# A field-interaction tower: one native product for the mixed tile, another order of the first loads, and two roundings on ScalarE

## What is computed

```python
e = jnp.stack([tbl_f[ids[:, f]] for f in range(39)], axis=1)      # (2048, 39, 16)
x = e
for W in (W0, W1):                                                # (128, 39*39), (128, 128*39)
    inter = (x[:, :, None, :] * e[:, None, :, :]).reshape(B, -1, 16)
    x = jnp.einsum('bid,hi->bhd', inter, W)
    outs.append(x.sum(axis=-1))
h = jnp.concatenate([*outs, dense_ctx], axis=1)                   # 128 + 128 + 16
h = jnp.maximum(h @ W_top1 + b_top1, 0.0)                         # 512
h = jnp.maximum(h @ W_top2 + b_top2, 0.0)                         # 256
y = h @ W_top3
```

## Time and profile before

| | |
|---|---|
| median of 3 runs | 783.21 us (782.36 to 785.63) |
| the profiled execution | 780.78 us, span from first to last instruction 779.0 us |
| TensorE (PE) busy | 696.8 us, 89% of the span |
| VectorE (DVE) busy | 674.9 us, 87% |
| GpSimd (POOL) busy | 501.0 us, 64% |
| ScalarE (ACT) busy | 420.2 us, 54% |
| moved by DMA | 115.67 MB, mean 148 GB/s |

### The profile page before, as it was taken

One profiled execution on the slowest core, in us unless ns is written; L12 is line 12 of the kernel. 1 busy time (PEld: TensorE's weight loads), 2 busy tenths in 40 slices (PEclk: granted clock), 3 DMA queues, 4 the chain that ended last, 5 costly groups with the idle time before them and its releaser, 6 DMA issues.

```text
span 779.0 us, 17028 instructions
## 1 busy us (share of the span) xinstructions
PE 696.8 (89%) x6210; PEld 595.1 (76%) x6210; DVE 674.9 (87%) x864; ACT 420.2 (54%) x769; POOL 501.0 (64%) x406
## 2 busy tenths in 40 slices
PE   0222678999999999999999999999999999999997
PEld 0222455878888888888888888888888888888887
DVE  5653999999999999999999999999999999888810
ACT  0001465656566656557565656655566656575741
POOL 6777887878787877868787887888787850000000
PEclk9999899999999999999999999999999999999999
DMA  4369569696867777787869796777867695854000
GB/s 101 90 156 275 129 184 164 164 171 170 163 167 168 131 185 130 187 134 190 161 163 168 173 162 169 171 148 182 141 171 142 162 160 138 162 153 133 13 7 1
DMA packets 171030, 115.67 MB, mean 148 GB/s; under 512 B 135043, under 2 KB 146906, under 8 KB 170563
## 3 DMA queue, kind: packets, MB, share of 16 engines
q1 hardware_dynamic: 154750, 108.80, 60.3%
q0 software_dynamic: 12800, 3.30, 6.6%
q10 hardware_dynamic: 3397, 2.47, 1.1%
HBM read 104.08 MB, written 15.53 MB: 154 GB/s over the span
## 4 chain that ended last, share of the span: by engine, by line
PE 77%; POOL 7%; DMA 4%; DVE 4%; issue 4%; SPq 3%; ACT 0%; DVEq 0%; ACTq 0%; POOLq 0%
PE z_ps L424 18%; PE x_ps L384 12%; PE x_ps L388 11%; PE x_ps L385 11%; PE g_ps L414 8%; POOL e_rows L360 7%; PE x1T_ps L445 4%; PE aux_ps L373 4%; PE x1T_ps L403 3%; PE x1T_ps L437 2%; SPq L280 2%; PE x1T_ps L435 2%; DVE product_lo L676 2%; DVE products L668 2%; DMA e_scratch<-e_d 2%
## 5 line engine op out<-in xcount | busy, mean ns | idle before, releaser
L360 POOL DMA_INDIRECT e_rows<-in_tbl_dram,ids_sb x400 | 500.6, 1252 | 134.7 <-issue 119.8
L514 ACT CAST product_hi<-products 117x1024 fp32r<-117x1024 f32 (+1 forms) x256 | 242.6, 948 | 102.7 <-DVE products L668 101.7
L676 DVE TENSOR_TENSOR product_lo<-products,product_hi 117x1024 fp32r<-117x1024 f32 (+1 forms) x256 | 277.4, 1084 | 23.1 <-ACT product_hi L514 22.9
L668 DVE TENSOR_TENSOR products<-bases 117x1024 f32<-117x1024 f32 (+1 forms) x256 | 277.5, 1084 | 7.1 <-DMA bases<-eT_scratch 6.5
L384 PE MATMUL x_ps<-product_hi,w_hi 117*128 117x512 f32 x448 | 198.5, 443 | 14.2 <-ACT product_hi L514 10.4
L424 PEld LDWEIGHTS z_ps<-G,w1T 128*128 128x128 f32 x1248 | 165.0, 191 | 17.3 <-issue 0.5
L385 PE MATMUL x_ps<-product_hi,w_lo 117*128 117x512 f32 x448 | 178.2, 398 | 0.0
L424 PE MATMUL z_ps<-G,w1T 128*128 128x128 f32 x1248 | 178.1, 280 | 0.0
L388 PE MATMUL x_ps<-product_lo,w_hi 117*128 117x512 f32 x448 | 148.5, 401 | 19.0 <-DVE product_lo L676 19.0
L388 PEld LDWEIGHTS x_ps<-product_lo,w_hi 117*128 117x128 f32 x448 | 84.3, 190 | 43.6 <-DVE product_lo L676 23.7
L384 PEld LDWEIGHTS x_ps<-product_hi,w_hi 117*128 117x128 f32 x448 | 85.6, 191 | 28.4 <-issue 13.8
(11 more groups left out here) (55 smaller groups left out, 340.1 us busy)
## 6 DMA issues: line engine op xcount, KB each, us to landing
bases<-eT_scratch SPq DMA_DIRECT2D x155, 468.0 KB
e_diag<-e_scratch SPq DMA_DIRECT2D x512, 10.0 KB
id_spread<-id_scratch SPq DMA_DIRECT2D x16, 437.5 KB
e_rows<-in_tbl_dram,ids_sb POOLq DMA_INDIRECT x400
e_scratch<-e_d SPq DMA_DIRECT2D x16, 320.0 KB, 9.5
eT_scratch<-e_rows SPq DMA_DIRECT2D x16, 312.0 KB
eT_scratch<-eT_scratch SPq DMA_DIRECT2D x16, 312.0 KB
w1T<-in_L_rec_W_dram SPq DMA_DIRECT2D x1, 2496.0 KB, 19.3
```

Source lines behind the costliest of these rows:

```text
L360: nc.gpsimd.indirect_dma_start(out=e_rows[t % E_SLOTS][:, f * D:(f + 1) * D], out_offset=None, in_=tables[f], in_offset=bass.IndirectOffse ...
L514: nc.scalar.copy(product_hi[:, first:first + count, :], products[:, first:first + count, :]).then_inc(hi_ready, 1)
L668: nc.vector.tensor_tensor(products[:, first:first + count, :], bases[u % 2][:, b:b + count, cols], bases[u % 2][:, a:a + 1, cols].to_broad ...
L676: nc.vector.tensor_tensor(product_lo[:, first:first + count, :], products[:, first:first + count, :], product_hi[:, first:first + count, : ...
```

## The change

Three edits. (1) Tile 3 is no longer split: its product stays float32 and goes into one float32 matmul with unsplit weights `w_native`, ahead of the other matmuls of group 1; ScalarE's rounding and VectorE's rest of that group shrink to one tile, 512 columns in place of 1024, and `multiply(g, 1)` waits until TensorE has read the product of the chunk before. (2) The first loads: those of chunk 0 are shared by SP (three) and ScalarE's queue (two), and SP issues those of chunk 1 when those of chunk 0 have landed. (3) `copy_e` moves from VectorE to ScalarE, and from the first chunk of the tile before to the end of its third; `store_e` moves in SP's list from chunk `c == 0` to `c == 3`; the rounding of the dense input moves to ScalarE too (`round_dense`). The weights' setup gets one more copy, 117 x 128.

```diff
+NATIVE = 3
...
+def parts_of(n):
+
+    _, _, count, first = GROUPS[n]
+    return slice(first, first + count - (first + count - 1 == NATIVE))
...
-        def load_base_part(queue, t, first, count, ready):
-            for a, starts in enumerate(BASES):
+            for a in range(begin, LOADS, step_of):
+                starts = BASES[a]
...
-            load_base_part(sp, 0, 0, HB // 2, first_ready[0])
+            load_base_part(sp, 0, 0, HB // 2, first_ready[0], 0, 2)
+            sp.wait_ge(first_ready[0], 16 * LOADS)
+            load_base_part(sp, 0, HB // 2, HB // 2, first_ready[1])
             for g in range(CHUNKS):
                 t, c = divmod(g, CPT)
...
                 if c == 0 and t + 1 < TILES:
                     store_eT(t + 1)
+                if c == 3 and t + 1 < TILES:
                     store_e(t + 1)
...
-                _, _, count, first = GROUPS[n]
+                parts = range(NT)[parts_of(n)]
+                if NATIVE == parts.stop:
+                    pe.wait_ge(product_ready, g * NG + n + 1)
+                    nc.tensor.matmul(x1_ps[:, :], w_native[:, :], products[:, NATIVE, :], start=False, stop=False)
                 pe.wait_ge(hi_ready, g * NG + n + 1)
-                for k in range(first, first + count):
+                for k in parts:
                     nc.tensor.matmul(x1_ps[:, :], w0_hi[:, k, :], product_hi[:, k, :], start=(k == 0), stop=False)
...
                 pe.wait_ge(lo_ready, g * NG + n + 1)
-                for k in range(first, first + count):
+                for k in parts:
                     last = nc.tensor.matmul(x1_ps[:, :], w0_hi[:, k, :], product_lo[:, k, :], start=False, stop=(k == NT - 1))
                 last.then_inc(contracted, 1)
...
-                _, _, count, first = GROUPS[n]
                 act.wait_ge(product_ready, g * NG + n + 1)
                 after(act, contracted, (g - 1) * NG + n + 1)
-                nc.scalar.copy(product_hi[:, first:first + count, :], products[:, first:first + count, :]).then_inc(hi_ready, 1)
+                nc.scalar.copy(product_hi[:, parts_of(n), :], products[:, parts_of(n), :]).then_inc(hi_ready, 1)
...
+            def copy_e(t):
+                act.wait_ge(gathered[t % E_SLOTS], (t // E_SLOTS + 1) * 16 * len(GATHERED))
+                act.wait_ge(looked_up, (t + 1) * sum(map(len, SETS)))
+                after(act, e_stored, 16 * t)
+                nc.scalar.copy(e_d[:, :, 0:F], e_rows[t % E_SLOTS][:, :].rearrange("b (f d) -> b d f", d=D)).then_inc(e_d_ready, 1)
+
+            def round_dense(t):
+                act.wait_ge(dense_loaded, (t + 1) * 16 * 3 * GAP // D)
+                after(act, h1_in_ps, M1 * t)
+                nc.scalar.copy(dense_parts[:, :], dense_now[:, :]).then_inc(dense_hi_ready, 1)
...
+            copy_e(0)
             act.wait_ge(eT_doubled, 16)
-            load_base_part(act, 0, HB // 2, HB // 2, first_ready[1])
+            load_base_part(act, 0, 0, HB // 2, first_ready[0], 1, 2)
...
+                if c == 1 and 0 <= t - 2 < TILES - 2:
+                    round_dense(t - 2)
                 if g < CHUNKS:
...
                 if g + 1 < CHUNKS:
                     round_products(g + 1, 1)
+                if c == 2 and t + 1 < TILES:
+                    copy_e(t + 1)
+                if g == CHUNKS - 1:
+                    round_dense(TILES - 2)
+                if g == CHUNKS + CPT:
+                    round_dense(TILES - 1)
...
+                if first + count - 1 == NATIVE:
+                    after(dve, contracted, (g - 1) * NG + n + 1)
                 nc.vector.tensor_tensor(products[:, first:first + count, :], bases[u % 2][:, b:b + count, cols],
...
-                _, _, count, first = GROUPS[n]
-                nc.vector.tensor_tensor(product_lo[:, first:first + count, :], products[:, first:first + count, :],
-                                        product_hi[:, first:first + count, :].bitcast(f32), ALU.subtract).then_inc(lo_ready, 1)
+                nc.vector.tensor_tensor(product_lo[:, parts_of(n), :], products[:, parts_of(n), :],
+                                        product_hi[:, parts_of(n), :].bitcast(f32), ALU.subtract).then_inc(lo_ready, 1)
...
+            nc.vector.tensor_copy(w_native[:, :], w0_sum[:, NATIVE, :]).then_inc(w0_split, 1)
...
-                if c == 0 and t + 1 < TILES:
-                    copy_e(t + 1)
```

More of the change, by code:

```diff
@@ L118, in cin_tower @@
         w0_lo = sb("w0_lo", [R, NT, H], f32r)
+        w_native = sb("w_native", [R, H])
         w1T = sb("w1T", [H, F, H])
@@ L235, in cin_tower, with load_base_part @@
         y_stored = sem("y_stored")
-        def load_base_part(queue, t, first, count, ready):
+        def load_base_part(queue, t, first, count, ready, begin=0, step_of=1):
             at = first % HB * D
-            for a, starts in enumerate(BASES):
+            for a in range(begin, LOADS, step_of):
+                starts = BASES[a]
                 step = starts[1] - starts[0]
@@ L483, in _ @@
                     look_up(t, n)
-            pe.wait_ge(w0_split, 2)
+            pe.wait_ge(w0_split, 3)
             for g in range(CHUNKS + 2 * CPT):
@@ L564, in _ @@
                               w0[j:j + count, 0:halves, shift, :]).then_inc(w0_loaded, 16)
+            copy_e(0)
             act.wait_ge(eT_doubled, 16)
-            load_base_part(act, 0, HB // 2, HB // 2, first_ready[1])
+            load_base_part(act, 0, 0, HB // 2, first_ready[0], 1, 2)
             round_products(0, 0)
-            act.wait_ge(w0_split, 2)
+            act.wait_ge(w0_split, 3)
             act.wait_ge(wt1_dense_split, 2)
@@ L607, in _ @@
         def _(dve):
-            def copy_e(t):
-                dve.wait_ge(gathered[t % E_SLOTS], (t // E_SLOTS + 1) * 16 * len(GATHERED))
-                dve.wait_ge(looked_up, (t + 1) * sum(map(len, SETS)))
-                after(dve, e_stored, 16 * t)
-                nc.vector.tensor_copy(e_d[:, :, 0:F], e_rows[t % E_SLOTS][:, :].rearrange("b (f d) -> b d f", d=D)).then_inc(e_d_ready, 1)
             def make_one_hot(t, n):
@@ L651, in split_dense @@
             def split_dense(t):
-                dve.wait_ge(dense_loaded, (t + 1) * 16 * 3 * GAP // D)
-                after(dve, h1_in_ps, M1 * t)
-                nc.vector.tensor_copy(dense_parts[:, :], dense_now[:, :]).then_inc(dense_hi_ready, 1)
                 dve.wait_ge(dense_hi_ready, t + 1)
@@ L726, in _ @@
             dve.wait_ge(w0_step, 1)
+            nc.vector.tensor_copy(w_native[:, :], w0_sum[:, NATIVE, :]).then_inc(w0_split, 1)
             nc.vector.tensor_copy(w0_hi[:, :, :], w0_sum).then_inc(w0_split, 1)
-            dve.wait_ge(w0_split, 1)
+            dve.wait_ge(w0_split, 2)
             nc.vector.tensor_tensor(w0_lo[:, :, :], w0_sum, w0_hi[:, :, :].bitcast(f32), ALU.subtract).then_inc(w0_split, 1)
@@ L734, in _ @@
                                     wt1_dense[2 * GAP:3 * GAP, :].bitcast(f32), ALU.subtract).then_inc(wt1_dense_split, 1)
-            copy_e(0)
             make_k_mask(1)
```

## The result

The changed kernel takes 798.44 us (median of 4 runs, 795.46 to 799.3), the kernel before 783.17 (4 runs, 782.36 to 785.63): a ratio of 1.0183, 95% interval 1.0148 to 1.0217. It is slower, and lies 14 us above the forecast of 784.5. The profiled execution took 795.46 us, span 793.6. A profile is one execution; ratios come from the medians.

What follows compares the result with a forecast made beforehand. TensorE was taken as the bound, VectorE's 3% slack just behind; -7.8 us at the start and +10.1 from chunk 12 on gave +2.3, the profiled 780.8 becoming about 783, as median 784.5; range 777 to 791.

Steps and rivals of the forecast that it cites:

- The regular part: From chunk 12 on, TensorE-bound: 52 chunks at +0.195 us each for the native product, +10.1 us.
- Rival (b): The float32 instruction costs what a float32r one does: 52 x -0.23 = -12 us, with the start 762 to 765; chance 0.08.
- Where the gains stop: Start: loads for chunks 4 and 8 limit VectorE's lead of 17 to 18 us; chunk 12 comes 7.8 us earlier.
- the first products: Chunk 0 needs half of the first loads' bytes, there at about 56 us, so it starts 6 us earlier.
- I take 6 of the 9: Tile 2's transposed rows: without `store_e`'s 9.12 us issue between their steps, the loads go out 6 us earlier, at 132.
- late next: Chunk 8, its loads without slack: complete at 146 us, so it starts 6.5 to 7 us earlier, at about 151.
- rival (d): Regular part gets a new wait, from `store_e` ahead of bases and `spread` or ScalarE's uncovered copy; 0.5 us gives 791; chance 0.15.
- (c): The start wins nearly nothing: SP's wait and w1T push tile 1's rows 4 to 5 us later; 789 us; chance 0.13.
- (a): A faster start: chunk 4's and 8's data 3 to 4 us earlier, -12 + 8, 777 to 779 us; chance 0.12.
- some 10 us: VectorE's new wait for bases before chunk 4, at 95 to 105 us, some 10 us long.

Runs made afterwards that it cites:

- e3: The native float32 product of tile 3 alone, put on the kernel before; 789.24 us, ratio 1.0104.
- e10: The changed kernel without SP's wait for chunk 0's loads (`first_ready[0]`); 792.94 us, ratio 1.0134.
- e11: The changed kernel with w1T issued at about 20 us and not at 73 us; 792.70 us, ratio 1.0129.
- e5: The changed kernel with w1T issued later, at g == 2, behind the loads of tile 1's bases; 798.27 us, ratio 1.0224.
- e1: The kernel before with only `copy_e` and the dense rounding moved to ScalarE and `store_e` to c == 3; 783.95 us, ratio 1.0036.
- e9: As e1, but `copy_e` at the end of the second chunk and `store_e` at c == 2; 781.92 us, ratio 1.0005 against the kernel before.
- e4: The changed kernel with the first loads as before, so only native product and copies; 788.85 us, ratio 1.0083 against the kernel before.
- e12: As e9, with w1T issued at about 20 us; first loads and split product as before the change; 778.39 us, ratio 0.9958 against the kernel before.

## Why the prediction was wrong

**The regular part** was right in kind and a little too dear. The float32 product is two instructions, 0.86 us for the pair in the chain (forecast 0.89; four passes at the float32r rate would be 0.92). The chunk costs 0.158 us more and not 0.195, so 8.2 us in place of 10.1. The Trainium skill ("FP8 and Floating Point Precision", TensorE Precision Notes) came closest: the estimate from its four passes was 0.85 and +0.16, and the trace agrees. Rival (b) is out. VectorE has its slack, 89% against the forecast 90, and its half microsecond a chunk wins little: in e3 chunk 12 begins 1.6 us earlier than before (200.3 against 201.9), and the 8 us come on top.

**The step that failed is the first half of "Where the gains stop"**: "the queue is full of bases until then anyway. I let the rows slip by 1 us for that, and take back as much for a queue that is emptier once they go". From it I had chunk 12 come 7.8 us earlier, at 194; it came at 208.5, 6.6 later, 14.4 us off. The 1.9 us too much for the regular part took some of it back; that leaves the 12.5 between the 783 forecast for a profiled execution and the 795.5 measured. Three things stood in its place:

- The queue was not full. In the 10 us of the wait it moved 127 GB/s where it had moved 232, and the bytes not moved passed later; e10 has 161, so the wait is a part of that and the longer list of loads the rest. e10: 4 us for the wait.
- I had moved w1T by 8 us and charged nothing. It moved by 11.7 (73.33 against 61.62) and so came to stand right ahead of the rows, whose store took 16.2 us to be complete in place of 5.3. It landed at 80.9 before, 1.1 us after the rows' store went out at 79.80, and at 91.3 in the changed kernel, 12.6 us after. e11: 4 us, and e5 shows that a later place moves the loss and doesn't end it. A load that nobody waits for had its price in those behind it.
- I gave the first products 6 us for half of the bytes. They got 2.7. I had counted ten loads of 234 KB from 48.72 on and overlooked five of 468 KB that go out behind SP's five (its ten in the earlier trace rows are five of each). Five loads took from 49.47 to 59.78, 10.3 us, where the first products had come 13.8 us after the first of fifteen loads, 48.72 to 62.49, with four times the bytes on their way. Bytes over bandwidth is no estimate for a few loads in flight. Nothing in my sum hung on the first products, but the wait ended at 59.8 and not at 56, which is the 3.7 us more of w1T's delay.

**The second failure is in the same part**: "part of that is the wait for the rows themselves, so I take 6 of the 9". The changed kernel shows 3.5 us of the 9 at tile 2 (8.14 from store to doubling against 11.59, with the rows going out 9.3 us later), e1 1.6, e9 0.3 and e4 nothing: most of `store_e`'s issue was cover for a store that was not complete. The "late next" that I named, chunk 8 without slack, was right, and with little won for tile 2's rows the lead of 5.8 us at chunk 4 in e1 was gone at chunk 8. In the changed kernel `spread(4)` adds 3.0 us of wait, since edit 3 put the store of `e_d` just ahead of it; my sentence on `store_e` in rival (d) saw the place but not this tile.

e4, without edit 2, shows this failure by itself: chunk 4 begins at 109.4, 7.2 us earlier than before, as forecast, but chunk 8 at 158.4, 0.6 later, where I had it at 151, and chunk 12 at 202.2. So there are two misses of like size. Edit 2 costs some 8 us that I had at nothing, and the 7.8 us of gain at chunk 12 are not there without it either; less 1.9 for the regular part, that is the 14 us.

**The rivals.** (c) had the right mechanism: the wait in SP's list and w1T behind it push tile 1's rows. I gave it 4 to 5 us at chunk 4 and 789 us; at the doubling it was 9.7 us (94.87 against 85.13), and SP's list carried 9.3 of it to tile 2's rows (130.95 against 121.67), a step that I did not follow. Its argument against, no idle time of the queue to lose, was the wrong one. (d) did not occur in the changed kernel, where chunk 60 begins 515.3 us after chunk 12, 7.5 more than before, edit 1's 48 x 0.158. In the profiles of e1 and e4, which have the same copies, waits for bases do stand in the regular part (24.3 and 16.9 us from 150 to 700 us, where there were 0.2); 5.8 us of e1's and 0.9 of e4's count between chunk 12 and 60. (a) fails for the changed kernel; e12, with w1T early, reaches 6.2 of its 12 us at chunk 12.

**What was right**: the wait at `copy_e` went, a wait of 10.67 us before chunk 4 took its place ("some 10 us"), and a smaller one, 5.53, stood before chunk 8; they stood 8 us later than forecast.

## What to carry to other kernels

Where one queue carries all loads, a transfer that nobody waits for is priced by what stands behind it: before a load is moved or held back, list the next small store or load that a chain needs, and see how many bytes come to stand ahead of it. A long issue between two dependent steps may only cover the wait for the first; read from the first step's landing, not from the issue's length, what taking it away brings. And put a large transfer where the queue has room, but expect a gain only where the queue is what the start waits for, and look at what the early place holds back: here the first loads, by 2.8 to 5.5 us. Last, compare each profile's time with the median of its kernel before reading a small difference from it.

## What the runs showed that I had not expected

- A float32 matmul of 117 x 128 weights and 512 columns holds TensorE 0.43 us an instruction and is two of them, 0.86; a float32r one 0.23. On TensorE three float32r matmuls (0.69) are cheaper than one float32.
- Five loads of 234 KB at once took 10.3 us, and 127 GB/s moved from 50 to 60 us, the gather's rows among them; with fifteen loads (4,680 KB) in flight it was 232 GB/s.
- A store of 312 KB takes 5.3 to 18.7 us from its issue to the step that waits for it; where it took 16.2 us or more, the 2.5 MB of w1T had been issued 3 to 5.4 us ahead of it.
- TensorE's granted clock fell with the idle start: this is the changed kernel from 100 to 110 us, and then the kernel before.

```profile
100.00:110.00 10.00, 9.14 (x52) 7.00 (x53) 2.60 (x4) 2.19 (x5) 7.64 (x8) 0.58 0.80 216
```

```profile
100.00:110.00 10.00, 8.21 (x73) 6.06 (x72) 9.97 (x13) 6.04 (x10) 8.30 (x6) 1.00 0.56 143
```

TensorE is shown busy 9.14 of 10 us with 52 matmuls at a mean clock of 0.58, near its lower level of 1.2 GHz, where it made 73 in 8.21 us at 2.4 GHz; in the 10 us ahead of it it had been busy 6.06. VectorE waited 10.67 us for bases up to 113.27, so this cost nothing that the runs show, but a busy share read without the clock would have called TensorE the bound there.
